# Rows of maxima into the stacked queries: VectorE and ScalarE copies on partitions 96 to 127 for a DMA

## The reference

```python
qh = (layernorm(x) @ Wq.T) / sqrt(16)          # 16 heads of 16
kh, vh = (ctx @ Wk.T), (ctx @ Wv.T)            # 154 keys
scores = einsum('bhqd,bhkd->bhqk', qh, kh) + rel    # relative term, distance clipped to +-4
scores = where(q >= k, scores, -1e30)
attn = softmax(scores, axis=-1)                # needs the row maximum of each query and head
x = x + tanh(g_xattn) * (einsum('bhqk,bhkd->bhqd', attn, vh) @ Wo.T)
# then x = x + tanh(g_ffn) * experts(layernorm(x)): 8 routed experts, 4 of them a row, and a shared one
```

## Time and profile before

| what | us |
|---|---|
| median of 3 runs | 708.72 (705.83 to 710.81) |
| the profiled execution | 711.47 |
| its span, first to last instruction | 709.4 |

### The profile page before, as it was taken

One profiled execution on the slowest core, in us unless ns is written; L12 is line 12 of the kernel. 1 busy time (PEld: TensorE's weight loads), 2 busy tenths in 40 slices (PEclk: granted clock), 3 DMA queues, 4 the chain that ended last, 5 costly groups with the idle time before them and its releaser, 6 DMA issues.

```text
span 709.4 us, 10602 instructions
## 1 busy us (share of the span) xinstructions
PE 612.7 (86%) x3352; PEld 478.7 (67%) x3352; DVE 444.1 (63%) x884; ACT 276.5 (39%) x501; POOL 194.1 (27%) x185
## 2 busy tenths in 40 slices
PE   2674969898989988968577999999999999999997
PEld 2553745566656754743356888888888888878886
DVE  3576656968597768740576674757657474665653
ACT  1442448334734465526151323334232333424222
POOL 2154004700362025300101232332323233232222
PEclk9876989899989998989768999999999999999999
DMA  6850132523252334472112122120212212031220
GB/s 207 231 138 16 28 67 78 127 50 82 53 140 45 74 67 117 94 237 51 24 27 91 29 76 75 35 83 31 90 59 80 68 42 81 26 90 60 78 72 30
DMA packets 37968, 55.89 MB, mean 79 GB/s; under 512 B 7888, under 2 KB 20048, under 8 KB 37904
## 3 DMA queue, kind: packets, MB, share of 16 engines
q1 hardware_dynamic: 37936, 55.49, 28.6%
HBM read 31.76 MB, written 4.85 MB: 52 GB/s over the span
## 4 chain that ended last, share of the span: by engine, by line
issue 41%; PE 32%; DVE 9%; POOL 8%; DMA 5%; ACT 3%; SPq 1%; POOLq 0%; DVEq 0%; ACTq 0%
POOL hl L1190 4%; PE oT L954 4%; PE work L969 4%; PE smax L891 3%; PE sT L934 3%; PE oT L958 3%; DMA qs<-mt 2%; DVE mx L621 2%; PE pg L1483 2%; PE pu L1483 2%; PE sT L933 2%; PE work L836 2%; PE py L1498 2%; POOL d L401 2%; PE work L867 1%
## 5 line engine op out<-in xcount | busy, mean ns | idle before, releaser
L1190 POOL TENSOR_TENSOR hl<-sg,hh 128x512 fp32r<-128x512 f32 x72 | 93.5, 1300 | 243.8 <-ACT hh L1233 240.7
L519 ACT ACTIVATE ex<-sT 128x512 f32<-128x512 f32 (+1 forms) x160 | 91.9, 593 | 143.5 <-PE sT L934 119.4
L1227 ACT ACTIVATE sg<-pg 128x512 f32<-128x512 f32 x72 | 43.1, 599 | 196.5 <-PE pu L1483 196.4
L621 DVE TENSOR_REDUCE mx<-smax 128x2 f32<-128x308 f32 x185 | 81.1, 473 | 34.4 <-PE smax L891 33.3
L891 PE MATMUL smax<-km,qs 96*128 96x308 f32 (+1 forms) x244 | 84.0, 379 | 18.1 <-DVE mx L621 11.5
L1498 PE MATMUL py<-wxl,hh 128*128 128x256 f32 x288 | 81.4, 283 | 5.3 <-DVE x L1377 4.1
L891 PEld LDWEIGHTS smax<-km,qs 96*128 96x128 f32 x244 | 46.6, 201 | 52.2 <-DVE mx L621 27.0
L1498 PE MATMUL py<-wxh,hl 128*128 128x256 f32 x288 | 80.5, 279 | 0.0
L1498 PE MATMUL py<-wxh,hh 128*128 128x256 f32 x288 | 80.3, 279 | 0.0
L1365 DVE TENSOR_TENSOR sg<-cwb,sg 128x512 f32<-128x512 f32 x64 | 58.9, 920 | 10.6 <-DMA cwb<-cwt_d 7.6
L1483 PE MATMUL pg<-x2l,wxh 128*128 128x512 f32 x144 | 60.8, 422 | 4.1 <-issue 4.1
(11 more groups left out here) (156 smaller groups left out, 1129.0 us busy)
## 6 DMA issues: line engine op xcount, KB each, us to landing
cwb<-cwt_d SPq DMA_DIRECT2D x64, 256.0 KB, 3.3
qs<-qh SPq DMA_DIRECT2D x64, 128.0 KB, 2.6
qs<-ql SPq DMA_DIRECT2D x32, 128.0 KB, 2.6
at<-rden_d SPq DMA_DIRECT2D x64, 64.0 KB, 2.3
out<-x SPq DMA_DIRECT2D x8, 512.0 KB, 4.4
ks<-km SPq DMA_DIRECT2D x16, 231.0 KB, 3.4
wx<-in_wx SPq DMA_DIRECT2D x9, 384.0 KB, 6.0
x<-in_x SPq DMA_DIRECT2D x3, 1024.0 KB, 8.5
```

What stands on the lines that cost most here:

```text
L519: nc.scalar.activation(ex[:, g % 2, i % 5, q0:HALF], ST[i % 2][:, q0:HALF], ACT.Exp).then_inc(exp_s, 1)
L621: nc.vector.reduce_max(mx[:, m_tile(h, p), stk::NSTK], banks[q % len(banks)][:, 0:PAIR].rearrange("p (j k) -> p j k", j=2), AX_X)\
L1190: nc.gpsimd.tensor_tensor(hl[:, i % R, :], sg[:, i % R, :], hh[:, i % R, :], ALU.subtract).then_inc(hl_done, 1)
L1227: nc.scalar.activation(sg[:, i % R, :], PG[i % RG][:], ACT.Silu).then_inc(sg_s, 1)
```

## The change

DVE writes the negative maxima into the last 32 columns of `nm`, which is now 128 wide for each of four tiles, its other columns zero. The transpose therefore puts the 32 rows on partitions 96 to 127 of the work bank, and DVE copies them straight to rows 96 to 127 of stack 0 of `qs`. ACT copies these 32 rows to the stacks 1 to 7, each by one copy of 32 partitions (`m_row`): stack 1 at the end of step 19 of the unit before, stacks 2 and 3 behind exp 0, 4 and 5 behind exp 1, 6 and 7 behind exp 2. Every stack holds all 32 rows (16 heads, high and low), and the selector picks the head: the contraction is over 128 rows. PE waits in step 0 for DVE's copy, and in the first and third step of each group for the copy of the stack it comes to. `mt`, its DMA and its semaphore are gone from SP's list; POOL has one more memset at the start.

```diff
--- before.py
+++ after.py
@@ -68,7 +68,8 @@
     k = np.arange(32)[None] - DIST
     put("band1", (p - k >= 0) & (p - k < DIST))
     put("causal1", np.where(k > p, NEG, 0))
-    put("head", (p >= 96) & (p < 100) & (p % 2 == np.arange(H)[None] % 2))
+    h = np.arange(H)[None]
+    put("head", (p >= 96) & (p % H == (h % 2) * NSTK + h // 2))
     put("mhalf", -0.5)
     put("eps", EPS)
     e = np.arange(E + 1)[None]
@@ -142,8 +143,7 @@
 
     kp = d0[0:96, :, :].rearrange("p h k -> p (h k)")[:, 0:NSTK * KL].rearrange("p (s k) -> p s k", s=NSTK)
     tp = sb("tp", [P, H, 32])
-    mx, nm = sb("mx", [P, NT, H]), sb("nm", [P, NT, 2 * H])
-    mt = sb("mt", [2 * H, HALF], F32R)
+    mx, nm = sb("mx", [P, NT, H]), sb("nm", [P, TU, P])
     raw_first = sb("raw_first", [P, NG, HALF])
     raws = (raw_first, raw)
     wq = raw[:, 0, :].rearrange("p (c d) -> p c d", c=C)
@@ -170,18 +170,19 @@
     q_ps, q_hi = sem("q_ps"), sem("q_hi")
     ks_in, k2_s, v_s = [sem(f"ks_in{g}") for g in range(NG)], sem("k2"), sem("v")
 
-    qs_in, ms_in = [[sem(f"qs_in{h}{part}") for part in range(2)] for h in range(2)], sem("ms_in")
+    qs_in = [[sem(f"qs_in{h}{part}") for part in range(2)] for h in range(2)]
     sm_ps, sx_s, mx_s = sem("scores_ps"), sem("sx"), sem("mx")
     relc_s, d_s, sadd_s, sub_s = sem("relc"), sem("d"), sem("sadd"), sem("sub")
     tp_s = sem("tile1_rest")
     sub0_s = sem("sub0")
-    nmh_s, nm_s, mT_ps, mT_s = sem("nm_hi"), sem("nm"), sem("mT_ps"), sem("mT")
+    nmh_s, nm_s, mT_ps = sem("nm_hi"), sem("nm"), sem("mT_ps")
+    m_first, m_rest = sem("rows_of_maxima_first"), sem("rows_of_maxima_rest")
     st_ps, exp_s, pv_ps, raw_s = sem("sT_ps"), sem("exp"), sem("pv_ps"), sem("raw")
     shift_in, den_out, den_in, rden_s, rden_out, rden_in = sem("shift_in"), sem("den_out"), sem("den_in"), sem("rden"), sem("rden_out"), sem("rden_in")
     at_s, y_ps = sem("at"), sem("y_ps")
 
     NI = 20
-    KS = 96 + 2 * 2
+    M_REST = NSTK - 1
 
 
 
@@ -272,13 +273,6 @@
         def k_stack(g):
             sp.dma_start(ks[0:96, 2 * g:2 * g + 2, :].bitcast(F32), km[:, 2 * g:2 * g + 2, 0:PAIR].bitcast(F32))\
                 .then_inc(ks_in[g], 16)
-
-        def m_stack(b, h):
-
-            q0 = HALF // 2 if h == 0 else 0
-            sp.wait_ge(mT_s, 2 * b + h + 1)
-            sp.dma_start(qs[96:KS, :, h * HALF + q0:(h + 1) * HALF].bitcast(F32), mt[:, q0:HALF].bitcast(F32))\
-                .then_inc(ms_in, 16)
 
         def divisors(u, h):
 
@@ -325,10 +319,7 @@
                 for part in range(2):
                     sp.wait_ge(qs_in[1][part], 16 * 6 * B)
                 load_weights()
-            if h == 0:
-                m_stack(b, 1)
-            elif ahead:
-                m_stack(b + 1, 0)
+            if h == 1 and ahead:
                 sp.wait_ge(st_ps, NI * (u + 1))
                 k_stack(NG - 1)
 
@@ -341,7 +332,6 @@
         sp.wait_ge(work_free, 12)
         for part in range(2):
             q_stack(1, part)
-        m_stack(0, 0)
         batches(sp, unit)
         divisors(2 * B - 1, 1)
 
@@ -350,6 +340,7 @@
         nc.gpsimd.memset(vb[:], 0.0).then_inc(pool_set, 1)
         nc.gpsimd.memset(tp[:], 0.0).then_inc(pool_set, 1)
         nc.gpsimd.memset(k2[:].bitcast(F32), 0.0).then_inc(pool_set, 1)
+        nc.gpsimd.memset(nm[:, :, 0:P - 2 * H], 0.0).then_inc(pool_set, 1)
         pool.wait_ge(w_in, 5 * 16)
 
         def rstd_of(u):
@@ -502,6 +493,13 @@
                 nc.scalar.copy(sx[:, m_tile(0, p), m_stacks(p).start + k, :], banks[q % len(banks)][:, 0:SW])\
                     .then_inc(sx_s, 1)
 
+        def m_row(u, h, stk):
+
+            q = slice(h * HALF + (HALF // 2 if h == 0 else 0), (h + 1) * HALF)
+            if stk == 1:
+                act.wait_ge(m_first, u + 1)
+            nc.scalar.copy(qs[96:P, stk, q], qs[96:P, 0, q]).then_inc(m_rest, 1)
+
         def raw_out(u, h, g):
             act.wait_ge(pv_ps, NG * u + g + 1)
             if not (isinstance(u, int) and u < 2):
@@ -517,6 +515,9 @@
                     act.wait_ge(pv_ps, NG * u + g - 1)
                 act.wait_ge(st_ps, NI * u + i + 1)
                 nc.scalar.activation(ex[:, g % 2, i % 5, q0:HALF], ST[i % 2][:, q0:HALF], ACT.Exp).then_inc(exp_s, 1)
+                if i < 3:
+                    for stk in (2 * i + 2, 2 * i + 3):
+                        m_row(u, h, stk)
                 if i == 4 and carry:
                     raw_out(u - 1, 1 - h, 3)
                 if i == 6 and ahead:
@@ -536,6 +537,8 @@
                     raw_out(u, h, i // 5 - 1)
                 if ahead and h == 0 and i == 19:
                     k_hi(b + 1, False)
+                if (h == 0 or ahead) and i == 19:
+                    m_row(u + 1, 1 - h, 1)
 
         x_hi(0, 0)
         q_out(0, 2)
@@ -550,6 +553,7 @@
                 q_out(1, 10)
             if m_tile(0, p) < 2:
                 near(0, p, M_START)
+        m_row(0, 0, 1)
         batches(act, unit)
         raw_out(2 * B - 1, 1, 3)
 
@@ -656,22 +660,25 @@
         def minus_max(b, h, start=False):
 
             r = slice(2 if h == 0 else TU, TU * (h + 1))
+            z = slice(2 - 2 * h, TU)
             dve.wait_ge(mx_s, 48 * b + (16 if h == 0 else 48))
             if not start:
                 dve.wait_ge(mT_ps, 2 * b + h)
-            nc.vector.tensor_scalar(nm[:, r, 0:H].bitcast(F32R), mx[:, r, :], -1.0, None, ALU.mult).then_inc(nmh_s, 1)
+            nc.vector.tensor_scalar(nm[:, z, P - 2 * H:P - H].bitcast(F32R), mx[:, r, :], -1.0, None, ALU.mult).then_inc(nmh_s, 1)
             dve.wait_ge(nmh_s, 2 * b + h + 1)
-            nc.vector.scalar_tensor_tensor(nm[:, r, H:2 * H], mx[:, r, :], -1.0, nm[:, r, 0:H],
+            nc.vector.scalar_tensor_tensor(nm[:, z, P - H:P], mx[:, r, :], -1.0, nm[:, z, P - 2 * H:P - H],
                                            ALU.mult, ALU.subtract).then_inc(nm_s, 1)
 
         def max_out(b, h, use, start=False):
+
             u = 2 * b + h
             q0 = HALF // 2 if h == 0 else 0
             dve.wait_ge(mT_ps, u + 1)
-            if not start:
-                dve.wait_ge(ms_in, 16 * u)
-            nc.vector.tensor_copy(mt[:, q0:HALF], W[use % 2][0:32, q0:HALF]).then_inc(mT_s, 1)
-            dve.wait_ge(mT_s, u + 1)
+            if not (isinstance(u, int) and u < 2):
+                dve.wait_ge(m_rest, M_REST * (u - 1))
+            nc.vector.tensor_copy(qs[96:P, 0, h * HALF + q0:(h + 1) * HALF], W[use % 2][96:P, q0:HALF])\
+                .then_inc(m_first, 1)
+            dve.wait_ge(m_first, u + 1)
             nc.vector.nop().then_inc(work_free, 1)
 
         def reciprocals(u):
@@ -900,7 +907,7 @@
             w = work(use_b, use)
             pe.wait_ge(nm_s, 2 * b + h + 1)
             for j in range(2 - 2 * h, TU):
-                last_one = nc.tensor.transpose(w[0:32, j * P:(j + 1) * P], nm[:, TU * h + j, :], ident)
+                last_one = nc.tensor.transpose(w[:, j * P:(j + 1) * P], nm[:, j, :], ident)
             last_one.then_inc(mT_ps, 1)
 
         def score(b, h, step, start):
@@ -910,7 +917,9 @@
             if not (start and step < 2):
                 pe.wait_ge(exp_s, NI * u + step - 1)
             if step == 0:
-                pe.wait_ge(ms_in, 16 * (u + 1))
+                pe.wait_ge(m_first, u + 1)
+            elif i in (0, 2):
+                pe.wait_ge(m_rest, M_REST * u + 2 * g + i // 2)
             if h == 0:
                 if step == 0:
                     pe.wait_ge(sub0_s, b + 1)
@@ -931,13 +940,13 @@
                 if h == 0:
                     for k in range(2):
                         nc.tensor.transpose(out[:, k * P:(k + 1) * P], sx[:, k, s, j * KL:j * KL + P], ident)
-                last_one = nc.tensor.matmul(out[:, q0:HALF], ks[0:KS, s, j * KL:j * KL + P], qs[0:KS, s, q], start=True,
+                last_one = nc.tensor.matmul(out[:, q0:HALF], ks[0:P, s, j * KL:j * KL + P], qs[0:P, s, q], start=True,
                                             stop=True)
             else:
                 if h == 0:
                     nc.tensor.transpose(out[:, P:2 * P], tp[:, 4 * g:4 * g + 4, :].rearrange("p h k -> p (h k)"), ident)
                 for k in range(2):
-                    last_one = nc.tensor.matmul(out[:, q0:HALF], k2[0:KS, 2 * g + k, :], qs[0:KS, 2 * g + k, q],
+                    last_one = nc.tensor.matmul(out[:, q0:HALF], k2[0:P, 2 * g + k, :], qs[0:P, 2 * g + k, q],
                                                 start=(k == 0), stop=(k == 1))
             last_one.then_inc(st_ps, 1)
 
@@ -1005,7 +1014,7 @@
         keys(0, -1, START + 4)
         values_in(0, -1, START + 7)
         transposes(1, -1, START + 8)
-        pe.wait_ge(pool_set, 5)
+        pe.wait_ge(pool_set, 6)
         pe.wait_ge(const_set, 5)
         for p in range(NM):
             if p == NM // 2:
```

## The result

The changed kernel takes 712.6 us (median of 20 runs, 705.5 to 718.4) against 708.7 us (median of 20, 704.4 to 712.0). Six of its 20 runs lie more than 1.5% above its fastest and count as a slower state; without them the ratio to before is 1.0041, 95% interval 1.0022 to 1.0061. A second set gave 1.0052 (1.0024 to 1.0080), 712.3 us. So it is slower by about half a per cent, inside "within 1%", but with the other sign than the forecast's 705.2 us and above the range of 699 to 711. One profile is one execution.

The account below looks back on a forecast made before the run. Second-half entries were taken as bound by the DMA of maxima, then ACT's chain. Unit 1 -3.3, units 3 and 5 +0.6, unit 7 -2.0, first halves +0.4, waits +0.8: -3.5 us, so 705.2 us; range 699 to 711.

Parts of the forecast that it names:

- within 1%: Whole kernel: the case of a time less than about 1% from before, 701.6 to 715.8 us; chance 0.76.
- Where the DMA waits stand, and what they give: Entries of units 1, 3, 5, 7: step 0 starts 4.2, 1.74, 1.74 and 2.43 us earlier, 10.1 us together.
- first-half entries: Entries of units 2, 4, 6: the projection covers the DMA, so its removal gains nothing there.
- The term of unit 7: Unit 7: step 0 starts 2.43 us earlier and exp 5 comes 2.0 us earlier, passed on to the experts' start.
- The price of the copies: ACT, seven copies a unit: overlapping starts cost 0.49 us per 512-column copy, 0.28 per 256-column copy.
- the copies do not overlap: Rival, behind exps 0 to 2 of every unit: copies cost 0.60 and 0.40 us, 5.5 us more, 710.7 us; chance 0.14.
- The Trainium skill's rule: ACT's SBUF-source copies expose their latency, 0.61 us for 512 columns, 0.40 for 256: sum some 5 us worse; not adopted.
- The cover in first halves is 0.9 us, and any dearer copy shows in full: First-half units, read on unit 6: copies use up 0.9 us of ACT's idle time; 0.1 us later each, 0.4 in all.
- the sum: All terms: -3.3 (unit 1), +0.6 (3 and 5), -2.0 (7), +0.4 (first halves), +0.8 (waits), giving -3.5 us.
- rival on the clock: Units 3, 5, 7 behind step 0: PE's clock falls to its lower level, 5.6 us lost, 710.8 us; chance 0.08.
- The added waits: PE waits for copies seven times a unit, nearly always already done: one exposed wait of 0.1 us a unit, 0.8 in all.
- the copies are free: Rival: ACT has room, so the whole 10.1 us less 0.8 for waits is won, 699.4 us; chance 0.18.

Follow-up runs that it names:

- switches: Kernel before plus eight short series of six ACT instructions in ACT's idle time ahead of unit 0, attention unchanged; one execution, no run time given.
- after_again: The changed kernel run again without edit, as a second set: 712.3 us, ratio 1.0052 to the kernel before.
- copies_moved: Changed kernel with copies of stacks 1 to 3 before the unit and 4 to 7 behind the `near` copies of tile 0: 704.8 us, 0.9946.
- after: The changed kernel's first set, median 712.6 us; its profiled execution took 718.3 us.
- no_copies_2: Changed kernel without ACT's seven copies and the waits for them; ACT writes zeros into stacks 1 to 7 before unit 0: 700.9 us, 0.9856.
- copies_moved_more: As copies_moved, but all seven copies of a first half lie before the unit: 701.5 us, 0.9897; repeated 703.0 us, 0.9908.
- copies_shared: As copies_moved_more, but POOL makes the copies of stacks 4 to 7 of all second halves: 702.5 us, 0.9896.
- copies_pool_last: As copies_moved_more, but POOL makes the copies of stacks 4 to 7 for unit 7 alone: 700.4 us, 0.9866.

## Why the prediction was wrong, step by step

**Where the DMA waits stand, and what they give: right.** From the end of `nm` to exp 0 the four second-half entries became shorter by 3.5, 1.8, 1.8 and 2.5 us (6.63, 6.25, 6.24, 7.04 became 3.14, 4.44, 4.44, 4.56). The forecast had 3.7 (exp 0 at 96.9 for 100.61), 1.74, 1.74 and 2.43. In units 3, 5 and 7 step 0 follows the projection, in unit 1 DVE's copy. The first-half entries did not gain; they lost, as told below. The term of unit 7 owed something to its one profile: in `switches` that entry took 6.25 us like those of units 3 and 5, not 7.04.

**The price of the copies: wrong, and this is the step that failed.** "Consecutive 512-column ACT operations start 0.49 us apart" is true of instructions on the same partitions. The forecast took it over to an alternation of 128 and 32 partitions, and took the two copies of L468, both on 96 to 127, as proof of it. The same answer of the timeline held the counter-proof, in the kernel before:

```profile
32.80 0.59 ACT L479 CAST xth<-work 128x512 fp32r<-128x512 f32 x1
33.41 0.62 ACT L468 CAST k<-cst 32x208 fp32r<-32x208 f32 x2
33.94 2.23 ACT L472 CAST ks<-cst 32x2464 fp32r<-32x2464 f32 x1
36.20 1.07 ACT L502 COPY sx<-smax 128x316 f32<-128x316 f32 x3
```

Coming from 128 partitions, L468 starts at 33.41, after the end at 33.39; the next on the same 32 start before the one ahead has ended (33.94 for 34.03); and the first copy on 128 partitions starts at 36.20, after 36.17. In an exp and two copies there are two changes and one pair on equal partitions: 0.62 + 0.53 + 0.63 = 1.78 us, 0.31 more than forecast, 0.93 in three such groups. In unit 3 the second pair of `near` copies came 11.84 us behind the end of `nm` (183.24 - 171.40) for 10.75 before (181.44 - 170.69), 1.1 later; forecast was 0.3. In unit 7 exp 5 came 1.15 us earlier behind the end of `nm` for the forecast's 2.0 (4.56 + 6.77 for 7.04 + 5.44); against `switches` (6.25 + 3.98), where no low clock lies there, it came 1.1 us later. That a count of the stretch instruction by instruction was the right method is shown by its other terms, which fit; the price of one pair was read off the wrong pair.

The rival "the copies do not overlap" named the price (0.60 and 0.40) and the point from which it decides (0.07 us a copy) and gave 710.7 us. It came near the measured time by luck: copies on equal partitions do overlap, and it priced every copy alike, where each change of partitions costs. The Trainium skill's rule ("VectorE: DVE Perf Modes", section "The TRN2 errata"), latency exposed between SBUF-source operations, is not borne out here as a distance of starts: a copy lasts the 0.61 us that it gives, but six copies from SBUF in a row on equal partitions start 0.52 us apart, and copies from PSUM lose the overlap as well when the partitions change.

**"The cover in first halves is 0.9 us, and any dearer copy shows in full": right as a rule, and it did.** Three groups of 1.35 us for the forecast's 1.05 brought exp 5 later by 0.9 to 1.5 us against its exp 0 in units 0, 2, 4 and 6 (5.65, 5.73, 5.46, 5.39 for 4.13, 4.52, 4.52, 4.48). In units 2 and 4 it was gone again by exp 7, where the normalised rows are waited for; in units 0 and 6 it stayed. The forecast's 0.1 a unit was therefore wrong in two ways, in price and in the assumption that all four units behave like unit 6.

**What nothing in the sum had: the low clock at other places.** Over attention as a whole the changed kernel has not more of it: PE's mean granted clock there is 0.95 in `after_again` and 0.92 in the profile before (0.95 in `switches`). But it lies elsewhere. In unit 0 PE gets less done in the 15 us behind exp 0 (75 matmuls for 90). The stretch of 15 us from exp 0 of unit 0 (columns as in the earlier trace rows), before, in `after_again`, and in `copies_moved`:

```profile
63.00:78.00 15.00, 13.84 (x90) 10.50 (x89) 9.55 (x27) 7.77 (x14) 2.63 (x3) 0.89 0.01 1
```

```profile
61.90:76.90 15.00, 14.14 (x75) 9.37 (x75) 8.03 (x23) 8.24 (x17) 2.67 (x3) 0.66 0.00 1
```

```profile
62.00:77.00 15.00, 13.81 (x90) 10.48 (x89) 9.53 (x27) 8.94 (x17) 2.66 (x3) 0.89 0.00 1
```

The granted clock of PE is 0.66 with copies behind exps 0 to 2, and 0.89 in the two others, without copies and with copies elsewhere. The lower of the two levels (1.2 for 2.4 GHz) lasted to 8 to 10 us behind exp 0 in the four profiles with copies there (`after` of the first set, `after_again` and the two with the DMA and copies), and to 2.5 to 5 us in the ten others. In unit 7 a stretch of it lay at the start before (first line) and 7 us behind exp 0 in the changed kernel (second line):

```profile
319.30:322.60 3.30, 3.30 (x12) 1.23 (x12) 0.00 (x0) 1.43 (x3) 0.00 (x0) 0.52 0.02 5
```

```profile
328.00:331.50 3.50, 3.50 (x13) 1.26 (x7) 0.00 (x0) 1.79 (x4) 0.00 (x0) 0.51 0.11 26
```

In `no_copies_2` unit 7 had none, and it ran from exp 5 to its end in 12.56 us for 14.18. The forecast's rival on the clock had units 3, 5 and 7 in view and 0.08. In `after_again` it was right about unit 7 only; in the profile of the first set also about unit 5 (0.52 in 262.5 to 266.0). In what part the low clock follows from PE's thinner work behind the copies, and what a profile owes to chance, I can't separate further: only the repetition over profiles speaks for a link, and that the thinner work is the cause isn't shown.

**What nothing in the sum had either: PE's wait for DVE at the entries of units 2, 4 and 6.** The forecast let the first-half entries be as they were, since the projection covers the DMA there. But step 0 of a first half also reads `sx`, from which DVE has to subtract the maxima of tile 1 first. The waits for it, before and in `after_again`:

```profile
PE sT L933 <- DVE sx L653: 8.1, 1, 8.1
```

```profile
PE sT L942 <- DVE sx L657: 14.3, 4, 8.0
```

One of them, 8 us long, is that of unit 0 in both. The other three are new, 6.3 us together. At the entry of unit 4 DVE's chain for tile 1 is itself held by POOL's `d`, which hangs on the `near` copies:

```profile
207.60 0.66 DVE L649 TENSOR_TENSOR sx<-sx,d 128x480 f32<-128x480 f32 x1 [0.98 <-POOL d L404]
...
213.23 0.43 PE L942 MATMUL sT<-idr,sx 128*128 128x128 f32 x2 [1.73 <-DVE sx L657]
```

From the end of `nm` to exp 0 these three entries took 7.42, 7.21 and 7.21 us for 6.14, 6.25 and 6.35 before, 0.9 to 1.3 longer. This is where ACT's delay in a second half reaches the next unit. Two such waits, 3.7 us together, are also there without any copies (`no_copies_2`), so they cap the gain as the normalised rows do.

**The added waits: seen, and mostly covered.** The waits of `after_again` (first fence) have three of PE for a copy of the rows, 3.3 us together where the sum had 0.8. All three are in first halves: 1.65 us before 140.44 in unit 2, 0.84 before 215.05 and 0.77 before 218.68 in unit 4; second halves have none. Most of it lies beside ACT, which is busy with the same copies: in unit 4 exps 0 to 3 start 1.36, 1.35 and 1.35 us apart without idle, while in unit 2 ACT waited 0.30 us for PE ahead of exp 2 (141.04 - 139.41 = 1.63 for 1.35). That 0.30 us is the only piece that I can lay on ACT's path, and no kernel took the waits away by themselves. Where POOL makes the copies, PE waits for them three times as well, 2.1 us together; with the copies moved ahead of the unit (copies_moved, copies_moved_more, copies_shared, copies_pool_last) no such wait is seen.

**The sum.** Forecast: 10.1 us gained by the DMA's removal, 5.8 paid for copies, 0.8 for waits, 3.5 left. By the ratios of the runs, 1.4% was gained (`no_copies_2`, 10 us) and 1.9% paid (from there to the changed kernel, 13 to 14 us). By the profiles of attention it was 8.0 gained (before to no_copies_2, 274.3 to 266.3; 6.0 from `switches`) and 13.6 paid (no_copies_2 to after_again, 266.3 to 279.9). Both say that the forecast's price was half of the real one or less, and this turned the sign. Whether the gain was sized too high isn't settled: the profiles say by 2 to 4 us, the runs say that it was right.

How much of the missing price is the distance of the starts? An estimate from the timelines: 0.31 us in the three groups of each second half and 0.30 in those of units 0 and 6, where the delay stays, are 5.5 us, and the forecast's 705.2 becomes 710.7. The sets measured 711.6 and 712.4 by their ratios (1.0041 and 1.0052 of 708.7). What the last 1 to 2 us are, the waits for tile 1 or the clock, stays open.

The rival "the copies are free" had 699.4 us, 0.987 of before; the kernels in which they are free, or nearly, measured 700.4 to 700.9 us, 0.9866 and 0.9856. The mechanism of the change is good, its placement on ACT was not.

## What to carry to other kernels

Before putting small instructions into an engine's stream, look in the trace for a pair that changes as the new pair will (partitions, source, operation) and take the pitch from that pair, not from a row of equal ones. On ACT keep instructions on one range of partitions together, and put those on another range where the engine waits anyway: with the same seven copies a unit, this change lost 0.5% with them at one place and gained 1% with them at another. And when a wait is taken away, write down what is late next: here the normalised rows stood 0.8 us behind the DMA in two of the four units.

## What was not expected of the hardware

- ACT overlaps an instruction with the one before it by about 0.1 us (six copies on equal partitions take 3.21 us, one takes 0.61), if both work on the same partitions. With a change of partitions the next starts 0.02 to 0.03 us after the end of the one before: 0.64 for 0.52 us from start to start with 512 columns from SBUF, 0.61 for 0.49 from PSUM. Two ranges of 32 partitions count as a change.
- A copy of 512 columns takes ACT 0.61 us whether it has 32 or 128 partitions. POOL takes (6.36 us)/7 = 0.91 us for one on 32 partitions, start to start.
- In the four profiles with copies behind exps 0 to 2 of unit 0, the clock of PE stayed at its lower level until 8 to 10 us behind exp 0, for 2.5 to 5 us in the ten others. Whether the copies are the cause isn't shown.
